# Reordering the head of a last stage: one output projection, one distance product and the expert bias

## The reference, cut to what matters

```python
out = jnp.einsum('bhts,bshd->bthd', attn, v).reshape(B, T, E)
return out @ out_proj_w.T + out_proj_b          # output projection
...
x = x + attention(layernorm(x), ctx, ...)       # x1 in the kernel
# routed layer on y = layernorm(x1); 32 prototypes, rank 16
x2 = jnp.sum(xf * xf, axis=1, keepdims=True)
p2 = jnp.sum(prototypes * prototypes, axis=1)
d2 = x2 + p2[None, :] - 2.0 * (xf @ prototypes.T)
dists = jnp.sqrt(jnp.maximum(d2, 0.0))
t = jnp.maximum(jnp.abs(temp), 0.1)
w = jax.nn.softmax(-dists / t, axis=1)
topw, topi = jax.lax.top_k(w, 2)
topw = topw / jnp.sum(topw, axis=1, keepdims=True)
# per chosen expert: h = B[idx] @ x, y = A[idx] @ h + bias[idx], weighted by topw
x = x + out
```

## Time and profile before

| | us |
|---|---|
| median of 3 runs (877.45 to 878.13) | 878.11 |
| the profiled execution's own time | 877.76 |
| its span, first to last instruction | 875.7 |
| busy PE / DVE / ACT / POOL in the span | 845.3 / 618.2 / 502.5 / 183.7 |

### The profile page before, as it was taken

One profiled execution on the slowest core, in us unless ns is written; L12 is line 12 of the kernel. 1 busy time (PEld: TensorE's weight loads), 2 busy tenths in 40 slices (PEclk: granted clock), 3 DMA queues, 4 the chain that ended last, 5 costly groups with the idle time before them and its releaser, 6 DMA issues. The chain is left out here.

```text
span 875.7 us, 20541 instructions
## 1 busy us (share of the span) xinstructions
PE 845.3 (97%) x8016; PEld 751.7 (86%) x8016; DVE 618.2 (71%) x1458; ACT 502.5 (57%) x1065; POOL 183.7 (21%) x237
## 2 busy tenths in 40 slices
PE   6999999999999999999999999999989987999998
PEld 6879889898898989899889998999878866888886
DVE  6686676677667766776676667666677667886874
ACT  4346666666666666666655666666666642444562
POOL 1050112011201121211112011211338536320000
PEclk9999999999999999999999999999999999999999
DMA  7976664656484737573856475655779322111011
GB/s 249 295 177 149 153 156 117 169 150 162 103 191 129 183 104 187 141 174 101 197 136 153 112 186 132 147 134 131 184 178 210 105 73 54 54 61 32 22 43 43
DMA packets 80481, 119.87 MB, mean 137 GB/s; under 512 B 8517, under 2 KB 59789, under 8 KB 80386
## 3 DMA queue, kind: packets, MB, share of 16 engines
q1 hardware_dynamic: 78402, 111.75, 50.7%
q0 software_dynamic: 1984, 6.82, 2.6%
HBM read 79.25 MB, written 39.28 MB: 135 GB/s over the span
## 5 line engine op out<-in xcount | busy, mean ns | idle before, releaser
L599 ACT ACTIVATE score_sb<-score_sb,neg_max 112x750 f32<-112x750 f32 x256 | 236.2, 923 | 71.5 <-DVE neg_max L780 68.5
L780 DVE CUSTOM_DVE_ANT_0 score_sb<-score_ps,neg_bias 112x750 f32<-112x750 f32 x256 | 239.1, 934 | 38.3 <-PE score_ps L988 32.5
L997 PEld LDWEIGHTS prob_ps<-ident,score_sb 112*125 112x125 f32 x1536 | 233.9, 188 | 20.7 <-ACT score_sb L599 4.4
L997 PE MATMUL prob_ps<-ident,score_sb 112*125 112x112 f32 x1536 | 246.3, 269 | 2.7 <-ACT score_sb L599 2.5
L608 ACT ACTIVATE probs_sb<-prob_ps 125x336 f32<-125x336 f32 x256 | 115.0, 449 | 191.7 <-PE prob_ps L997 189.8
L790 DVE COPY probs_sb<-prob_ps 125x336 f32<-125x336 f32 x256 | 129.0, 504 | 120.9 <-PE prob_ps L997 119.2
L984 PE MATMUL score_ps<-k_st,q_st 97*112 97x512 f32 x256 | 105.2, 411 | 0.5 <-DMA q_st<-q_parts 0.5
L925 PE MATMUL acc<-ctx_hi,w_hi 128*128 128x376 f32 (+1 forms) x256 | 92.7, 362 | 7.3 <-DVE ctx_lo L815 6.7
L492 POOL COPY rsum_wide<-rsum 112x256 f32<-112x256 f32 x32 | 12.7, 398 | 381.0 <-DVE rsum L799 381.0
L925 PE MATMUL acc<-ctx_lo,w_hi 128*128 128x376 f32 (+1 forms) x256 | 92.0, 359 | 0.0
L925 PE MATMUL acc<-ctx_hi,w_lo 128*128 128x376 f32 (+1 forms) x256 | 90.2, 352 | 0.0
(11 more groups left out here) (189 smaller groups left out, 1554.8 us busy)
## 6 DMA issues: line engine op xcount, KB each, us to landing
k_st<-k_parts SPq DMA_DIRECT2D x96, 375.0 KB
k_parts<-kq_parts SPq DMA_DIRECT2D x60, 188.0 KB, 2.3
k_parts<-kq_parts SPq DMA_DIRECT2D x60, 187.0 KB, 3.8
q_st<-q_parts SPq DMA_DIRECT2D x96, 112.0 KB
ctx_raw<-in_ctx_t SPq DMA_DIRECT2D x14, 752.0 KB, 6.6
q_parts<-kq_parts SPq DMA_DIRECT2D x30, 224.0 KB, 2.3
xb<-in_x SPq DMA_DIRECT2D x8, 448.0 KB, 5.5
attn_t<-attn SPq DMA_DIRECT2D x32, 112.0 KB, 2.0
```

Of the source, the lines that this page charges most:

```text
L599: nc.scalar.activation(scores[:, w % NSC, :], scores[:, w % NSC, :], ACT.Exp, bias=neg_max[:, w % UB:w % UB + 1], scale=-1.0, accum_out=su ...
L780: nc.vector.tensor_tensor_reduce(out=scores[:, w % NSC, :], in0=score_ps[:, at:at + S], in1=neg_bias[:, w // HG % TC, :], scale=1.0, scala ...
L997: last = nc.tensor.transpose(prob_ps[j][0:SW, s * TW:(s + 1) * TW], scores[:, w % NSC, (BT * j + s) * SW:(BT * j + s + 1) * SW], ident[0:T ...
```

## The change

On PE, `project_out` of batch 4 moves from in front of the last three `down` products of batch 0 to behind `transpose_y(1)`; `distances(1)` moves from behind `transpose_routes(0)` to in front of it. The wait on `small_ready` is replaced by a wait on a new semaphore, `bst_parts_ready`, which stands behind `distances(1)` and in front of `transpose_routes(0)`. On DVE, `small_later` is cut in two: `temperature` stays in front of `routing(0)`, and `bias_parts` goes behind the residuals of batch 4, which themselves go behind `routing_weights(0)` and `yt_low(1)`. On ACT, `norm` is cut into `yt_high` and `row_squares`; for batch 1 `yt_high` goes ahead of the second `copy_h(0, 1)`, and `copy_h(0, 0)` ahead of the exponential. From b = 1 on the loop is what it was.

```diff
@@ ACT
+            def yt_high(b):
                 eng.wait_ge(y2_ready, b + 1)
                 for c in range(TC):
                     eng.wait_ge(yt_ps_ready, TC * b + c + 1)
                     ...
+            def row_squares(b):
...
             distance_root(0)
+            copy_h(0, 0)
             eng.wait_ge(small_ready, 1)
             second_weight(0)
-            copy_h(0, 0)
+            yt_high(1)
             copy_h(0, 1)
             widen_route(0)
-            norm(1)
+            row_squares(1)
@@ DVE
-            def small_later():
+            def bias_parts():
                 eng.wait_ge(bst_ready, 1)
                 for r in range(4):
                     ...
+                last.then_inc(bst_parts_ready, 1)
+
+            def temperature():
+                eng.wait_ge(small_loaded, 16 * 5)
...
             routing_dot(0)
             normalise(1)
-            small_later()
+            temperature()
             routing(0)
+            routing_weights(0)
+            yt_low(1)
             residual(EARLY + 1, 0)
             residual(EARLY + 1, 1)
-            routing_weights(0)
-            yt_low(1)
+            bias_parts()
@@ PE
             transpose_dot(0)
-            for c in range(TC):
-                project_out(EARLY + 1, c)
             down(0, 0, 1)
             down(0, 1, 0)
             down(0, 1, 1)
             transpose_y(1)
-            eng.wait_ge(small_ready, 1)
+            for c in range(TC):
+                project_out(EARLY + 1, c)
+            distances(1)
+            eng.wait_ge(bst_parts_ready, 1)
             for b in range(LAST):
                 ahead = b + EARLY + 2
                 transpose_routes(b)
-                distances(b + 1)
+                if b:
+                    distances(b + 1)
```

More of the change, by code:

```diff
@@ L1140, in finish @@
         bst_ready = sem("bst_ready")
+        bst_parts_ready = sem("bst_parts_ready")
         small_step = sem("small_step")
@@ L1234, in deviation @@
                 nc.scalar.activation(sd[:, :], veps[:, :], ACT.Sqrt).then_inc(sd_ready, 1)
-            def norm(b):
+            def yt_high(b):
                 eng.wait_ge(y2_ready, b + 1)
@@ L1274, in experts @@
                 nc.scalar.activation(g_hi[:, :, :], gated[:, :, :], ACT.Copy).then_inc(g_hi_ready, 1)
-            norm(0)
+            yt_high(0)
+            row_squares(0)
             eng.wait_ge(pt_loaded, 16)
@@ L1307, in _ @@
                 if b + 2 < B:
-                    norm(b + 2)
+                    yt_high(b + 2)
+                    row_squares(b + 2)
             eng.wait_ge(y_ps_ready, TC * (LAST - 1) + 1)
@@ L1334, in small_later @@
                     if r % 2 == 0:
-                        nc.vector.tensor_copy(bst[rows, :], bst_hi[rows, :].bitcast(F32))
+                        last = nc.vector.tensor_copy(bst[rows, :], bst_hi[rows, :].bitcast(F32))
                     else:
-                        nc.vector.tensor_tensor(bst[rows, :], bst_raw[rows, :], bst_hi[rows, :].bitcast(F32),
-                                                ALU.subtract)
+                        last = nc.vector.tensor_tensor(bst[rows, :], bst_raw[rows, :], bst_hi[rows, :].bitcast(F32),
+                                                       ALU.subtract)
+                last.then_inc(bst_parts_ready, 1)
+            def temperature():
+                eng.wait_ge(small_loaded, 16 * 5)
                 nc.vector.tensor_scalar(t_neg[:, :], temp_col[:, :], -1.0, 0.1, ALU.mult, ALU.max)\
```

## The result

Fifteen executions of the changed kernel have a median of 880.53 us (878.45 to 881.80), fifteen of the kernel before 878.13 us; the ratio is 1.0023 with a 95% interval of 1.0013 to 1.0032. The change makes the kernel slower by 2.0 us, 1.1 to 2.8. The forecast was 878.7 us with 875.6 to 880.2 around it; the ratio on before's 878.13 us gives 880.15 us, within by 0.05 us, and the bare median of 880.53 us lies 0.3 us outside.

The account below looks back on a forecast made before the run. PE was taken as the last stage's bound, with a 5.01 us hole. The restart at 745.3 plus 2.45, 2.78 and 1.0 gave 751.5 against 750.87, 0.6 us later: 878.7 us on the median, range 875.6 to 880.2.

Parts of the forecast that it names:

- The new wait: PE's wait before the turned routes of batch 0 for the bias parts: PE idles 5.2 us, 740.1 to 745.3.
- the hold: While POOL works, DVE instructions with SBUF operands alone wait for POOL's current instruction to end, one to one.
- PE and DVE up to there: Last stage's head: batch 1 rows turned until 732.5, projection ends 738.2, distances end 740.1, routes ready 738.2 against 743.5.
- The size of the hold: Bias parts on DVE, from 740.0: end at 745.3 if POOL holds them, 742.3 if nothing does.
- From the routes to the point: Turned routes to first projection half of batch 5: 745.3 + 2.45 + 2.78 + 1.0 = 751.5, 0.6 us later.
- the point: Measuring point, the end of batch 5's projection half on PE, 750.87 before; changes there go on to the end in full.
- The hand-over through `gate(0)`: Turned routes, second half of gate and hand-over before batch 5's projection: 2.45 us at the low clock.
- The clock: Low clock lasts 4.4 us after PE restarts; 1.95 us fall into the projection half and cost 1.0.
- Rival D: Wait for `gate(0)` breaks PE's stretch; low clock through the whole projection half, 5.1 us: 880.1 us, chance 0.14.
- A: The forecast: time only moves from a wait for routes to one for bias; 878.7 us, 877.3 to 879.7, chance 0.47.
- B: Bias parts not held by POOL: 875.8 us, or 873.9 if the clock stays up; chance 0.23.
- C: Bias parts partly held, DVE getting two turns at a stroke, PE starting near 744: 877.4 us, chance 0.13.

Follow-up runs that it names:

- bias in the idle time: Changed kernel with the four bias instructions moved between routing(0) and routing_weights(0), where DVE idles and POOL does nothing: 873.88 us, ratio 0.9948 to the kernel before.
- POOL waiting: Changed kernel with POOL's split of batch 5 made to wait for the bias parts: 878.23 us, ratio 0.9999 to the kernel before.
- bias behind the gate: Changed kernel with the bias instructions behind gated_low(0) on DVE and PE's wait at the first bias matmul of up(0, 0): 873.85 us, ratio 0.9943 to before.
- PE's wait alone: Changed kernel with PE's bias wait moved to the first bias matmul of up(0, 0), bias work still before gate(0): 879.84 us, ratio 1.0014 to before.
- changed again: The changed kernel itself, unaltered, measured and profiled once more in a later session: 880.57 us, ratio 1.0016 to the kernel before.
- in two halves: Changed kernel with two bias instructions before routing_weights(0), two behind gated_low(0), and PE's wait in up(0, 0): 874.59 us, ratio 0.9947 to before.
- the hole filled: Changed kernel with 38 unused matmuls added on PE between distances(1) and the wait for the bias parts: 878.09 us, ratio 0.9997 to before.
- the bias late in the order of before: Kernel before with only the bias instructions moved behind gated_low(0) and PE's wait for them in up(0, 0): 879.23 us, ratio 1.0003 to before.

## Why the prediction was right in kind and short in size

**The new wait.** Right. It was forecast that the gain of the head (routes early) is given back in full by a wait for the bias parts, which POOL holds; PE idled 5.51 us in place of 5.01. Undoing the hold in two ways (bias in the idle time, POOL waiting) brought the four instructions from 5.82 to 2.24 us. The forecast had rows of 2 to 4 elements for the hold; the changed kernel shows it for 512 as well, for the cast (2.04 us beside POOL, 0.41 with POOL idle) and for the subtraction with two SBUF inputs (1.66 and 0.68). But the forecast's sentence on DVE instructions with SBUF operands alone is wider than the traces. In before the reciprocal L58 took 0.14 us at 726.25, inside `at_lo` (725.79 to 727.88), and the reciprocal L1411 0.17 us at 739.07, inside the first addition (from 738.96). With the bias behind the gate two `stats` (L47, 512 elements) took 1.26 us at 743.43 beside POOL's additions (742.85 to 745.39), as long as at 748.44 with PE's wait alone and POOL idle. What the two engines meet at is not shown, only which lengths and ends go together.

**PE and DVE up to there.** Right within 0.3 us by the stage's own clock: in "changed again" the turned rows of batch 1 at 15.3 us (forecast 15.2), the first bias instruction at 23.4 (23.5).

**The size of the hold.** Short by 0.4 us: the last bias instruction ended at 29.2 us of the stage, forecast 28.8; the four took 5.82 us from the first start to the last end, forecast 5.3. Most of that is in the forecast's own sum: with its own lengths the turns give 742.8 + 0.69 + 1.25 + 0.2 + 0.69 = 745.6, not 745.3.

**From the routes to the point.** The hand-over through `gate(0)` took 2.57 us, forecast 2.45. The clock is the term that was mis-sized: the projection half took 4.55 to 4.64 us, forecast 3.8. 0.25 of that is that a half which starts behind a wait takes 3.02 us even at the full clock, not 2.78 (3.02 at a granted clock of 1.00 with the bias behind the gate, in the idle time, in two halves and with the hole filled); 0.55 is the clock, since the low clock lasted about 6 us past PE's new start and not 4.4. Of the 1.3 us that the forecast missed 0.4 is the hold, 0.1 the hand-over, 0.25 the start behind a wait and 0.55 the clock. The 4.4 was one execution's figure of before, carried over: in the earlier trace rows the clock is 0.50 until 748.0 and 0.91 in the microsecond behind, so it went up near 748.2, 4.6 us past 743.55. How far one execution speaks for another can be estimated from the clock rows of the runs in which PE was busy without a break behind its last hole: 4.6 us in before, 4.1 with PE's wait alone (rows below; PE started again at 748.31), 5.7 with the bias late in the order of before, 6.1 with POOL waiting. In the two profiles of the changed kernel it was 6.1 and 6.0.

```profile
750.00:752.00 2.00, 2.00 (x6) 1.41 (x6) 1.25 (x4) 0.66 (x2) 0.00 (x0) 0.50 0.65 207
752.00:753.00 1.00, 1.00 (x5) 0.56 (x3) 0.00 (x0) 0.00 (x0) 0.00 (x0) 0.80 0.00 0
```

**Rival D.** Its time, 880.1 us, is what was measured, and its condition, a low clock for more than 6 us past the new start, was met within the reading (6.1 and 6.0). Its reason, that the wait for `gate(0)` breaks PE's stretch, is not shown: the low clock lasted 6.1 us without that break too (POOL waiting). And its sum came out in part by luck: no run shows the 2.55 us that it doubles for a half at the full clock (2.78, or 3.02 behind a wait), though its 5.1 agrees with 12 of the 0.43 us between the starts of projection matmuls at a granted clock of 0.50 (changed kernel, 749.60 to 752.16); and the projection half took 4.6 us and not 5.1 (5.46 where it was at the low clock throughout, POOL waiting), and the hold, which D took from A, made up for it with 0.4. The forecast, A, had the waits right, but its own range ended at 879.7, and by its chances a measurable loss had 0.15. That the time lies inside the full range, by 0.05 us on the ratio, is luck.

**The rivals.** B (not held) and C (partly held) are out. That DVE or POOL could not follow PE later did not come about in the changed kernel: behind the point PE's chain has no hole.

**What stays open.** Why the low clock lasted 6 us in the changed kernel and 4.6 in before was not found, nor which activity of PE keeps or brings back the clock; the profile of "POOL waits" shows only that it can be lost (1.00 until 744.0, 0.50 from 745.5) with no hole longer than 2.2 us.

## What to carry to other kernels

When work is pushed to "last", look at what stands behind it in its own engine's list and what another engine does at that moment: here 2.2 us of DVE work became 5.8 beside POOL and stood in front of the one instruction that everything waited for. Moving the wait to the use was worth next to nothing until the work was moved too; moving both turned a loss of 2.0 us into a gain of 5. And an experiment that gets rid of a hole should be priced with the clock behind it, 1.3 to 2.0 us for a hole of 5 us here, but only as far as no other engine is just behind.

## What the runs showed that I had not expected

A wait added on POOL made the kernel 2 us faster than the changed one. The start of the last stage varied between 716.1 and 719.5 us over the twelve profiles, though the code in front of it is the same; this is as large as the effect studied, and only times counted from the stage's start made the profiles comparable. And the clock's cost was smaller where PE's holes were filled than the sum over slow matmuls says (2.3 us added, 1.3 to 1.5 paid in the kernel before), since DVE was only that far behind.
